# A drain on GpSimd behind every four row gathers of a four-layer graph network

## The reference

```python
x = layernorm(x + L0(x, edge_attr_32))
x = layernorm(x + L1(x, edge_attr_17))
x = layernorm(x + L2(x))          # two hops of the normalized adjacency
x = layernorm(x + L3(x))          # one hop, and a 96x96 weight

# L0, twice, with leaky_relu behind each:
msg = x[src] @ W_msg + edge_attr @ W_edge
agg = segment_max(msg, dst)
agg + x @ W_root + b
# L1:
w   = relu(edge_attr @ W1.T + b1) @ W2.T + b2
agg = segment_sum(w * x[src], dst)
relu(x @ Ws.T + bs + agg @ Wn.T + bn)
# L2, L3: segment_sum(norm * h[src], dst)
```

## Time and profile before

| what | value |
|---|---|
| time, median of 3 runs | 5110.67 us (5105.8 to 5115.91) |
| the profiled execution's own time | 5120.4 us |
| span of the profile | 5118.6 us |
| mean granted clock of PE | 0.785 of full speed |
| busy, share of the span | PE 79%, PEld 52%, DVE 44%, ACT 20%, POOL 50% |
| GpSimd's gathers of L709 | 2496, of which 832 in each pass |
| DMA | 695.04 MB, on the mean 136 GB/s |

### The profile page before, as it was taken

One profiled execution on the slowest core, in us unless ns is written; L12 is line 12 of the kernel. 1 busy time (PEld: TensorE's weight loads), 2 busy tenths in 40 slices (PEclk: granted clock), 3 DMA queues, 4 the chain that ended last, 5 costly groups with the idle time before them and its releaser, 6 DMA issues.

```text
span 5118.6 us, 56111 instructions
## 1 busy us (share of the span) xinstructions
PE 4044.6 (79%) x19316; PEld 2656.8 (52%) x19316; DVE 2232.8 (44%) x5877; ACT 1002.8 (20%) x2108; POOL 2581.0 (50%) x2689
## 2 busy tenths in 40 slices
PE   5777767677368776777764998998898969999999
PEld 4333333333333333333333655555555649999999
DVE  3454555555124444444443555555555552222211
ACT  1100000000122222222223333333333330001101
POOL 4666666665556666666655665566566530000000
PEclk9999999999965667666655566556666559999999
DMA  5333333333234444444432443434343327777776
GB/s 136 100 99 89 102 95 100 89 101 88 48 93 136 124 135 127 137 121 138 131 100 66 117 122 114 123 115 123 110 127 108 117 84 268 269 266 268 263 260 219
DMA packets 251432, 695.04 MB, mean 136 GB/s; under 512 B 80458, under 2 KB 163082, under 8 KB 219914
## 3 DMA queue, kind: packets, MB, share of 16 engines
q1 hardware_dynamic: 56126, 348.35, 21.2%
q0 software_dynamic: 85568, 131.83, 12.0%
q10 hardware_dynamic: 109516, 212.06, 11.4%
HBM read 477.94 MB, written 214.09 MB: 135 GB/s over the span
## 4 chain that ended last, share of the span: by engine, by line
PE 59%; another core or an unknown queue 14%; DVE 12%; issue 10%; ACT 2%; DMA 1%; POOL 1%; DVEq 0%; ACTq 0%; POOLq 0%; SPq 0%
PE banks L1118 17%; PE banks L981 9%; PE banks L1022 7%; PE banks L976 6%; PE banks L956 6%; PE banks L947 5%; PE banks L995 5%; DVE scan L1831 5%; DVE hot_lo L1483 3%; DVE hot_hi L1485 1%; PE banks L735 1%; DVE hot_key L1848 1%; DVE hot_src L1850 1%; ACT adj L1350 1%
## 5 line engine op out<-in xcount | busy, mean ns | idle before, releaser
L709 POOL DMA_INDIRECT gath<-table,ids x2496 | 2406.3, 964 | 1425.4 <-issue 698.5
L1831 DVE TENSOR_TENSOR_SCAN scan<-keep_of,scan,banks 96x512 f32<-96x512 bf16 x621 | 791.3, 1274 | 1737.9 <-remote 972.9
L1118 PE MATMUL banks<-r_parts,adj_in 128*128 128x288 bf16 x7203 | 890.2, 286 | 5.1 <-DVE r_parts L1531 2.6
L1118 PEld LDWEIGHTS banks<-r_parts,adj_in 128*128 128x128 bf16 x7203 | 883.2, 142 | 7.4 <-DVE r_parts L1531 3.4
L995 PEld LDWEIGHTS banks<-ident,scan 96*128 96x128 f32 x2496 | 400.9, 224 | 911.7 <-issue 505.7
L995 PE MATMUL banks<-ident,scan 96*128 96x96 f32 x2496 | 528.4, 359 | 325.7 <-DVE scan L1831 254.5
L981 PE MATMUL banks<-ea_of,w_edge_of 32*96 32x512 f32 x832 | 765.1, 1016 | 0.3 <-issue 0.3
L1022 PE MATMUL banks<-hot_key,hot_src 128*128 128x392 bf16 x1600 | 543.3, 475 | 272.8 <-issue 139.3
L1332 ACT ACTIVATE back<-banks 128x384 f32<-128x384 f32 x624 | 305.2, 489 | 2062.0 <-remote 873.4
L1848 DVE TENSOR_SCALAR hot_key<-iota_key,key_t 128x392 bf16<-128x392 int16 x1600 | 505.4, 316 | 21.0 <-ACT key_t L1371 21.0
L956 PEld LDWEIGHTS banks<-w_edge_out,hid 97*128 97x128 f32 x1664 | 320.2, 287 | 307.2 <-issue 305.4
(11 more groups left out here) (158 smaller groups left out, 2100.9 us busy)
## 6 DMA issues: line engine op xcount, KB each, us to landing
adj_in<-adjacency SPq DMA_DIRECT2D x147, 1568.0 KB
scanned_rows<-back ACTq DMA_DIRECT2D x153, 768.0 KB
adjacency<-adj ACTq DMA_DIRECT2D x100, 784.0 KB
gath<-table,ids POOLq DMA_INDIRECT x2496
ea_of<-in_ea_t SPq DMA_DIRECT2D x78, 512.0 KB
keep_of<-keep_max_d SPq DMA_DIRECT2D x52, 768.0 KB
keep_of<-keep_sum_d SPq DMA_DIRECT2D x26, 768.0 KB
table<-x_sb SPq DMA_DIRECT2D x10, 240.0 KB, 4.4
```

Of the source, the lines that this page charges most:

```text
L709: pool.indirect_dma_start(gath[:, b, t, :], None, tables[p][:, :], bass.IndirectOffsetOnAxis(ap=ids[:, 1, n:n + 1], axis=0),).then_inc(s_g ...
L1118: m = pe.matmul(sum_ps[:, u, j, :], adj_in[:, a, :, h], r_parts[:, n % 2, h, :, :].rearrange("p k f -> p (k f)"), start=h == 0, stop=h == ...
L1831: ve.tensor_tensor_scan(scan[0:D, b, at:at + Q], keep_of[:, i % 2, CHUNK * b + at:CHUNK * b + at + Q], turn_ps[k % 2], start, keep_op, tak ...
```

## The change

One line is added to GpSimd's program in the second branch: a `drain` behind the four gathers of each quarter, ahead of the next quarter's wait. It carries no semaphore. It is built and executed 26 pairs x 2 chunks x 4 quarters x 3 passes = 624 times. No other instruction is added, removed or moved on any engine; a line of the old kernel from L713 on stands one line lower in the new one.

```diff
@@ -710,6 +710,7 @@
                                         gath[:, b, t, :], None, tables[p][:, :],
                                         bass.IndirectOffsetOnAxis(ap=ids[:, 1, n:n + 1], axis=0),
                                     ).then_inc(s_gath[4 * b + k], 16)
+                                pool.drain()
 
                     all_pairs(gather_pair)
                     nodes(p)
```

## The result

The changed kernel takes 6735.95 us (median of 4 runs, 6730.59 to 6749.64) against 5108.24 us before. The ratio is 1.319 (95% interval 1.3162 to 1.3219): 1628 us slower. The forecast was 5149 us, in a range from 4900 to 5230.

The account below looks back on a forecast made before the run. In passes 0 and 1 no engine was full; GpSimd's back-to-back gathers were taken to hold up PE's results. Drains add 17.6 us in pass 0 and 20.6 in pass 1, +38 in all: 5149 us, range 4900 to 5230.

Parts of the forecast that it names:

- I take 0.14 us: Cost assumed for each drain behind GpSimd's gathers, read from the only drain in the profile, behind an integer ramp.
- my upper bound of 0.99: Most a drain was expected to add, in us: a 1.29 us pause in place of the usual 0.305 between gathers.
- the count of 273: Quarters of passes 0 and 1 (126 and 147) without a real GpSimd wait, where each drain was to count in full.
- The second rival: Dear drain on GpSimd, up to 0.99 us each: 5381 us, or 5175 if PE's results get through; chance 0.15.
- also lets the results through: Dear-drain case where PE's results come on time: GpSimd's quarter 5.99 us without other waits, +65 us, 5175 us.
- turning point of 0.83 us: Drain cost at which letting PE's results through stops paying: 5.0 + 0.83 us is what a quarter takes now.
- my own signs: Profile signs for each case: idle time ahead of each fourth gather, scan waits, quarter times; pass 2 within 10 us.
- none of the four: The cases: small loss (0.34), faster by releasing PE's results (0.33), no change (0.18), dear drain (0.15).
- PE bounds that pass: Claim that in pass 2 GpSimd's 281.9 us of waiting hide the drains' 18 us, so they add 0.
- The reading of before: While GpSimd issues gathers back to back, others see PE's results late, about 1 to 2.7 us after it falls silent.
- the first rival: Drains let PE's results through in passes 0 and 1, so real waits go: 4940 us, 4857 in full; chance 0.33.
- The shortest [silence] that did was 1.29 us: Shortest GpSimd pause seen to let PE's results through; pauses of 0.305 us never did. Argued against a faster kernel.

Follow-up runs that it names:

- e2: The changed kernel with two drains in place of one behind each quarter's gathers: 6753.92 us.
- e7: The kernel before, with GpSimd writing an unread integer ramp of 800 columns behind each quarter's gathers, no drain: 5023.56 us, ratio 0.9829.
- e19: The changed kernel, unedited, measured again where before takes 4440.45 us: 6676.79 us, ratio 1.5021.
- e8: The changed kernel with each drain replaced by a wait until the gathers of the quarter before have landed: 5198.09 us, ratio 1.017.
- e1: The changed kernel with each drain replaced by a semaphore wait until the quarter's own four gathers have landed: 6338.43 us, ratio 1.2518.
- e9: The changed kernel with the edge attributes' load split into two transfers and the restart marks' load cut to 64 columns from each pass's third pair: 6138.89 us.
- e11: The kernel before, with an unread integer ramp of 400 columns on GpSimd behind each quarter's gathers, no drain: 4649.75 us, ratio 1.0476.
- e12: The kernel before, with an unread integer ramp of 800 columns on GpSimd behind every second quarter only, no drain: 4649.03 us, ratio 1.0472.
- e17: Repeat of the kernel before with an unread 400-column ramp on GpSimd behind each quarter's gathers, no drain: 4650.68 us, ratio 1.0458.

## Why the prediction was wrong

- **"What a drain behind a gather costs no row shows … I take 0.14 us": the step that failed.** A drain behind gathers waits until they have landed. Its price is 3.92 - 0.305 = 3.6 us on the mean, 26 times what I took and 3.7 times my upper bound of 0.99. The bound was read from waits for PE's results, which are no limit for a transfer. The profile's page of before gave 4.4 us from issue to landing for another transfer (`table<-x_sb`), and 4.4 us would have been the better upper end. The drain's own price, 0.03 to 0.06 us (e2), is below my value.
- **"Where GpSimd goes into a real wait, the drain runs in the wait's place": the count of 273 failed with it.** All 621 drains between quarters show, the least with 2.36 us of idle time: once a quarter takes 8.6 us, GpSimd has no wait for PE left in which a drain could hide (the next gather starts 0.7 to 1.04 us behind each drain).
- **The second rival had the mechanism, not the size.** I wrote "until the last gather is wholly out of GpSimd" and stopped at its descriptors. Its form "also lets the results through" is what happened: a quarter of 5.0 + 3.6 = 8.6 us in pass 0, where I had 5.99. The drain is 4.3 times its turning point of 0.83 us. By my own signs none of the four fits, since pass 2 changed by 469 us.
- **"PE bounds that pass": the cover of pass 2 failed** by size alone. A gather takes 0.972 us on the mean there and not the median's 0.944, so GpSimd's own quarter was 5.1 us, and 1.3 of the 6.4 us could be hidden. The drain added 3.5, the pass went from 6.38 to 8.65 us a quarter, and 469 us came out.
- **The reading of before holds, with a limit.** With the drains the scan never waits for "remote" (973.9 us before), and with a pause of 1 us alone those waits become shorter and the kernel 1.7% faster (e7). So the first rival's effect exists, though no run ties the 1.7% to it. The limit is that GpSimd's gathers without a stop are not enough to hold PE's results up: at the 4441 level 28 of them in `nodes` do not (e19). What else it takes is open.
- **The sum, redone.** 621 x (3.92 - 0.305) = 2245 us is what the drains put into GpSimd's program. Where nothing is held up, the whole of it shows: 6677 - 4440 = 2236 us. That is the check. Where before takes 5108, it also has 668 us of hold-up by the inference above, and the changed kernel keeps 50 to 59 of them (6726 and 6736 less 6677). The drains so take away about 614, and 2245 - 614 = 1631 us is left, 1628 measured. This second step is bookkeeping: its 614 come from the same times as the 1628, so their agreement says no more than the first step's does.
- **"The shortest [silence] that did was 1.29 us"** was no lower limit: 1.0 us lets results through as well (e7), in part. Below that nothing was measured at that level.

## What to carry to other kernels

A drain on GpSimd behind gathers is a wait for the newest of them: price it as landing time plus restart, with what other loads do to the landing (2.5 to 9 us here), not by a drain behind arithmetic. If what you want is a pause, put in one that waits for nothing, and if older rows are all you need, wait for an older transfer (e8: 87 us in place of e1's 1270). A gain that rests on removing a hold-up must be tested where the hold-up is absent: the pause that gave 1.7% should cost there, as its shorter form did by 4.6% (the 1 us form was not measured there).

## What the runs showed of the hardware that I had not expected

- A drain on GpSimd covers the indirect DMAs that it has issued: it ends 0.47 us after their last packet at the least, 0.55 at the median, and never before (621 drains).
- One kernel had two levels of time, 5068 to 5112 and 4441 us, the same through a group of experiments, and no profile taken at the faster one (e9, e11, e12, e17 to e19) shows any engine waiting for "remote", not even beside the 28 gathers, 1.25 us apart, of `nodes`. Whether before itself looks so there was not seen.
- A load of 512 KB whose outermost dimension has two entries goes out in two strands. With a load of 768 KB right behind it, the gathers that met the two landed 4 to 6 us later than others (8.76 and 6.21 us of idle time against 2.5). Written as two transfers of 32 partitions it cost them about 2 us less each (6.50 and 4.25).
